# A longer ring for the row gathers of a routed expert layer: 24 slots in place of 6

## The reference, cut to what matters

```python
xt = _layernorm(x)                               # 1024 tokens x 256
logits = xt @ Wr.T + bias                        # 16 experts
topk_val, topk_idx = top_k(softmax(logits), 2)
w = topk_val / (sum(topk_val) + EPS)
y[t, e] = (silu(xt @ Wg[e]) * (xt @ Wu[e])) @ Wd[e]      # Wg, Wu 256x128; Wd 128x256
routed[t] = sum over the two chosen e of w * y[t, e]
shared = silu(xt @ sWg) * (xt @ sWu) @ sWd
x = x + tanh(g_ffn[1]) * (routed + shared)
```

## Time and profile before

| | us |
|---|---|
| runs: median (lowest to highest of 3) | 526.02 (524.07 to 526.48) |
| profiled execution | 522.03 |
| its span, first to last instruction | 520.2 |
| busy in the span: TensorE matmuls | 464.4 |
| VectorE | 374.2 |
| ScalarE | 186.4 |
| GpSimd | 147.8 |

### The profile page before, as it was taken

The page is one execution under the profiler, slowest core; times in us unless marked ns, Lnnn a source line. Parts: engine busy times, 40 slices in busy tenths (PEclk is TensorE's granted clock), DMA queues, the critical chain, the costliest instruction groups (busy, mean ns, idle before and its releaser), DMA issues.

```text
span 520.2 us, 8732 instructions
## 1 busy us (share of the span) xinstructions
PE 464.4 (89%) x3033; PEld 380.5 (73%) x3033; DVE 374.2 (72%) x877; ACT 186.4 (36%) x386; POOL 147.8 (28%) x140
## 2 busy tenths in 40 slices
PE   4699999999999999998999989999899966999800
PEld 4468668667666689997888878888689955888600
DVE  6979889889889774679777857676884569444423
ACT  3324232233142350242442235555470231566500
POOL 4835001101104000162663002222300123765064
PEclk9899999999999979999999999999989968999955
DMA  7402202202401300000211104335080111567444
GB/s 262 135 1 82 81 1 81 81 3 77 141 24 56 139 1 2 0 1 30 62 31 52 54 21 138 110 124 178 1 323 11 42 42 34 152 179 130 124 123 130
DMA packets 20701, 42.39 MB, mean 81 GB/s; under 512 B 3808, under 2 KB 11232, under 8 KB 20672
## 3 DMA queue, kind: packets, MB, share of 16 engines
q1 hardware_dynamic: 18416, 35.84, 20.4%
q0 software_dynamic: 2256, 6.16, 5.5%
HBM read 35.83 MB, written 6.16 MB: 81 GB/s over the span
## 4 chain that ended last, share of the span: by engine, by line
PE 60%; issue 17%; DVE 12%; POOL 6%; DMA 3%; ACT 1%; POOLq 0%; SPq 0%; DVEq 0%
PE ps L537 11%; PE ps L539 11%; PE ps L538 11%; PE ps L689 8%; PE ps L951 5%; PE ps L966 3%; POOL COMB L514 3%; POOL probs L409 2%; PE ps L585 2%; PE ps L637 2%; PE ps L595 1%; DMA X<-x 1%; PE ps L942 1%; PE ps L566 1%; PE ps L558 1%
## 5 line engine op out<-in xcount | busy, mean ns | idle before, releaser
L409 POOL TENSOR_TENSOR probs<-probs,rowrec 128x512 f32<-128x512 f32 x28 | 28.6, 1043 | 169.2 <-DVE rowrec L1405 168.9
L1021 ACT ACTIVATE PT_hi<-ps 128x512 fp32r<-128x512 f32 (+1 forms) x64 | 35.7, 601 | 58.1 <-PE ps L595 52.8
L537 PE MATMUL ps<-xs_hi,A_hi 128*128 128x512 f32 x128 | 52.6, 411 | 1.5 <-DVE xs_lo L1358 1.5
L539 PE MATMUL ps<-xs_hi,A_lo 128*128 128x512 f32 x128 | 50.7, 396 | 0.0
L538 PE MATMUL ps<-xs_lo,A_hi 128*128 128x512 f32 x128 | 50.6, 395 | 0.0
L1367 DVE TENSOR_TENSOR PT_lo<-ps,PT_hi 128x512 fp32r<-128x512 f32 (+1 forms) x64 | 41.7, 686 | 7.3 <-ACT PT_hi L1021 7.0
L537 PE MATMUL ps<-N_hi,PT_hi 128*128 128x256 f32 x128 | 36.4, 284 | 0.0
L539 PE MATMUL ps<-N_hi,PT_lo 128*128 128x256 f32 x128 | 36.2, 283 | 0.0
L538 PE MATMUL ps<-N_lo,PT_hi 128*128 128x256 f32 x128 | 36.2, 283 | 0.0
L504 POOL DMA_INDIRECT XG<-xd,index x31 | 29.7, 958 | 22.1 <-DVE index L1716 8.1
L1393 DVE TENSOR_REDUCE rowmax<-ps 128x8 f32<-128x512 f32 x32 | 21.8, 682 | 17.7 <-PE ps L585 17.7
(11 more groups left out here) (198 smaller groups left out, 1193.6 us busy)
## 6 DMA issues: line engine op xcount, KB each, us to landing
WX<-ffn SPq DMA_DIRECT2D x16, 384.0 KB, 6.1
W<-attn SPq DMA_DIRECT2D x8, 704.0 KB, 4.1
W<-attn SPq DMA_DIRECT2D x8, 672.0 KB, 4.0
W<-attn SPq DMA_DIRECT2D x16, 320.0 KB, 4.3
yd<-Y SPq DMA_DIRECT2D x31, 128.0 KB
WF<-ffn SPq DMA_DIRECT2D x8, 384.0 KB, 3.9
X<-x SPq DMA_DIRECT2D x4, 256.0 KB, 4.9
xd<-qb SPq DMA_DIRECT2D x2, 512.0 KB, 3.4
```

The lines of the kernel that those rows point to most:

```text
L409: nc.gpsimd.tensor_tensor(part, part, rowrec[:, 4 * h:4 * h + 4, :].unsqueeze(3).to_broadcast([P, 4, 2, L]), ALU.mult).then_inc(s.p, 1)
L537: nc.tensor.matmul(dst, lhs[0], rhs[0], start=start, stop=False)
L539: return nc.tensor.matmul(dst, lhs[1], rhs[0], start=False, stop=stop)
L1021: return nc.scalar.activation(dst, src, ACT.Copy)
```

## The change

One constant. The slot count of `XG` goes from 6 to 24; the wait on `ro.xT` in `gather_rows` then begins at b = 24 and asks for block b - 24; `Y` begins 18 slots (18 KB per partition) further on, and `XG` with `Y` then take 55 of the 56 slots of 1 KB that the space has. Transposes keep their place two blocks ahead of gate_up.

```diff
 BLOCKS1 = 2 * TOK // P + E1 - 1
 RING = 8
-XROWS = 6
+XROWS = 24
```

## The result

The kernel after takes 553.26 us (median of 4 runs, 549.44 to 555.19), the kernel before 526.25 (524.07 to 528.2, 4 runs, one more than in the table of before). The forecast was no change, 523.2 to 528.0.

What follows compares the result with a forecast made beforehand. The prediction took TensorE, full from 446 to 485.5 us, to bound the routed blocks. All terms summed to 0 us, so the median would stay at 526.0 us, range 523.2 to 528.0.

Steps and rivals of the forecast that it cites:

- What bounds the kernel: First to last row gather: TensorE busy throughout 446 to 485.5 us, 1.625 us a block; the removed wait is GpSimd's.
- The ring wait: GpSimd's gathers from block 6: without it all go out every 1.25 us, the last 4.8 us earlier; 0 us on path.
- What TensorE gets from it: Rows from block 18 on arrive earlier but were never late, with 2.0 us of slack at block 30; 0 us.
- B's row wait: Sign that the forecast is wrong: TensorE waits for a gather after block 1.
- A's shorter time: Sign that the forecast is wrong: the time drops by over 2.6 us.
- the line on TensorE being busy all of 446 to 485.5 us: Expected in the trace after the change: TensorE still busy for that whole stretch.
- Empty blocks: Gathers of blocks 23 to 30, served every 1.97 us; slack at block 30 grows from 2.0 to 4.2 us; 0 us.
- The stores: Stores of `Y` share the DMA engines with faster gathers; 0 us, at best a gain of a few tenths.
- the moved tile: `Y` moves by 18 slots; its place in memory does not matter to ScalarE's copies; 0 us.
- GpSimd beside VectorE: Gather issue beside VectorE's block operations: no contention seen; by the skill's rule 1.54 us a gather, still 0 us.
- Rival A: Late empty-block gathers stall TensorE in unprofiled executions; the change takes back at most 3.99 us, to 522.0 us; chance 0.05.
- Rival B: Empty-block gathers slow each other; with doubled service TensorE would stall 9.6 us, to 535.6 us; chance 0.03.

Runs made afterwards that it cites:

- keep6: Kernel after, with its 24 slots and moved `Y`, but gather b again waits for TensorE's transposes of block b - 6; 528.42 us, ratio 1.0022.
- paced24: Kernel after, with GpSimd clearing an unread tile of 256 columns after each gather, gathers 1.45 us apart; 536.69 us, ratio 1.0212.
- slower24: Kernel after, with two clears after each gather, the second waiting for the first, gathers 1.72 us apart, last seven 2.04; 528.23 us, ratio 1.0034.
- pool_rows: Kernel after, with GpSimd issuing plain loads of rows in order in place of indirect gathers, so another output; 518.98 us, not comparable with other totals.
- sp_rows: Kernel after, with SyncE loading rows in order in place of indirect gathers, result gathers plain too, so another output; 507.32 us, not comparable.

## Why the prediction was wrong, point by point

- **What bounds the kernel**: right for the execution that I read, and read too narrowly. TensorE was full from 446 us on, with gathers 1.25 us apart until block 17, and I took that as proof that this rate is harmless. Other executions with the waits of a ring of 6 are not so lucky: the profile of `keep6` has waits of TensorE of 2.2 and 1.4 us, and the profiled execution of before was 3.99 us under the median. One profile was a sample from a spread. That the slower executions of the kernel before lose their time in the same way is likely and not shown, as no slower one has a profile here.
- **The ring wait, "on the path: 0 us"**: this is the step that failed. GpSimd's side came out to the tenth up to block 28 (465.3 forecast for block 23; 466.05 measured with a start 0.7 later). But I priced the wait by who is behind it on its own engine. It also kept the rate of gathers at TensorE's pace from block 18 on, and cut the burst whenever TensorE fell behind. Without it: 27 us between the medians. The same step took TensorE's 1.625 us a block as given beside faster gathers, and so also its transposes of blocks 0 to 6 as done some 20 us before GpSimd asks for them: blocks 5 and 6 were taken up as done at 474 and 480 us.
- **"What TensorE gets from it"**: right, it never waited for a row after block 1, and so had nothing to gain. Neither of the two signs named for being wrong came (B's row wait, A's shorter time). What told was the line on TensorE being busy all of 446 to 485.5 us.
- **Empty blocks**: no row after block 1 was late, so that term did not matter. The trace of the kernel after gives no landing times for its gathers, so whether they take 1.97 us each at this rate was not seen.
- **The stores, the moved tile**: right; `keep6` shows the place to be free.
- **GpSimd beside VectorE**: I looked at how long each instruction takes, and these are as before (946 ns for a gather, 288 for VectorE's). The harm does not show in any instruction's length; it is in the time between one's end and the next one's start. The rule of the Trainium skill that I weighed ("SBUF — State Buffer", section "SBUF: two separate sides") has VectorE holding GpSimd up; no run shows that, and what was measured goes from GpSimd's gathers to steps out of TensorE.
- **Rival A** suspected stalls near the gathers in the 3.99 us above the profile, which `keep6` makes likely, but blamed rows. The rings of 5 and 4 have ratios 0.3 and 0.4% under 1, the first with an interval that touches it; that a shorter burst is the reason is not shown.
- **Rival B** was on the right side by luck, for a wrong reason: TensorE would have waited for rows. It got 0.03, and the price of 9.6 us was a third of the real one.

What stays open: by which path indirect gathers hold up the handovers out of TensorE, and alone those. TensorE starts at once when VectorE has finished and its work is taken up late; whether its products finish late or only their steps arrive late can't be told, since the ends of matmuls are modelled. Whether the recording of the profile takes part can't be said either.

## What to carry to other kernels

A wait that costs its own engine's idle time may be the brake on something that harms others: before removing it, ask what its engine will do more of, and how fast. In a kernel like this one, hold GpSimd's indirect gathers to the pace at which they are used, by a short ring (here four to six slots), and don't send them ahead. One profile of a kernel whose runs spread by 0.5% shows one draw; look for the spread's cause before a stretch is called undisturbed.

## What the runs showed of the hardware

- Indirect gathers of 128 rows of 1 KB, issued every 1.25 us, delay handovers out of TensorE by up to 25.7 us in the kernel after, taken up in order and mostly 4.2 us apart, for as long as they go on; at 1.45 us TensorE still waits some 11 us over 31 gathers (`paced24`), at 1.72 not at all but for rows (`slower24`).
- Plain loads of the same size from GpSimd, every 0.54 us (`pool_rows`), and from SyncE (`sp_rows`) do no harm to TensorE.
- A stall costs a second time through the clock: the granted clock was 0.50 from 459 to 485.5 us in the kernel after, also while TensorE worked again; the mean gate and up product took 410 ns against 380, and TensorE's work in the routed blocks 7.7 us more.
